# Leaving the last four item groups of a graph-attention edge pass out of gathers, sums, scores and products

## The chip, the cores and the metric

The kernel runs on one core of one Trainium2 chip. The metric is the device time of one execution in microseconds (us): the median of several runs, of the whole program from its first to its last instruction with what the runtime puts around it. Beside the runs stands one execution that the hardware profiler recorded. A measurement of this kernel is repeated and its median compared with that of the kernel before.

## The reference, cut to what matters

A graph-attention layer with a residual, then a layer of experts with a residual. The change touches the attention over the edges only:

```python
def _L0_gnn_ref(x, edge_index, edge_attr, W_l, b_l, W_r, b_r, att, bias):
    N, E, D, H, C = (2500, 40000, 256, 8, 32)
    NEG_SLOPE = 0.2
    n = x.shape[0]
    x_l = (x @ W_l + b_l).reshape(n, H, C)
    x_r = (x @ W_r + b_r).reshape(n, H, C)
    src, dst = (edge_index[0], edge_index[1])
    x_j = x_l[src]
    g = jax.nn.leaky_relu(x_r[dst] + x_j, NEG_SLOPE)
    alpha = jnp.einsum('ehc,hc->eh', g, att)
    alpha = alpha + jnp.log(edge_attr)[:, None]
    amax = jax.ops.segment_max(alpha, dst, num_segments=n)
    ex = jnp.exp(alpha - amax[dst])
    denom = jax.ops.segment_sum(ex, dst, num_segments=n)
    alpha = ex / (denom[dst] + 1e-16)
    out = jax.ops.segment_sum(x_j * alpha[..., None], dst, num_segments=n)
    return out.reshape(n, H * C) + bias
```

The input has 6250 nodes of 256 features and 100,000 edges, sorted by `dst`. So a run of consecutive edges belongs to one node, and a tile of 128 edges touches few tiles of 128 nodes.

## The kernel before, in words

`build` runs one block after another: `prepare` (layer norm, the two projections, the list of items), `edges` (the attention), `route` (second layer norm, gate, slots of tokens), `experts`, `combine`. Between two blocks all engines meet. The change lies in `edges` and in `pipeline`, which lays out its work.

**Items, groups, chunks.** An item is one tile of 128 edges paired with one tile of 128 nodes that it touches. Items come in pairs of edge tiles (`PAIR` = 2). There are `EB` = 391 such pairs and `NODE_TILES` = 49 tiles of nodes; a pair needs one more item pair each time the node tile changes, so at most 2 x (391 + 48) = 878 items can exist. `ITEMS` rounds this up to 896. Four items are a group (`G`), so there are `GROUPS` = 224 groups, and 32 items, or 8 groups (`TURN`), are a chunk: 28 chunks. The last chunk is groups 216 to 223; groups 220 to 223 hold items 880 to 895, which is above 878. Items that do not exist are padding: their weights come out as zero.

**What a group needs.** In the order of the data:

- POOL gathers the left rows of the group's sources, four indirect DMAs (`gather`, L749), 16 groups ahead at most (`RINGS`): it waits on `weighed` of the group 16 back.
- SP loads the right rows of the node tiles (`load_rights`, L764) and the local node numbers (`load_locals`, L771), and for each chunk the marks of runs (`load_chunk`, L781).
- ACT makes the one-hot matrix (`part` L984, `one_hot` L990); PE sums right and left rows (`sum_rows`, L1087 and L1089, in two halves); ACT rectifies (`rectify`, L976).
- DVE multiplies with the attention vector and reduces to scores (`scale` L821, `put_linear` L826, `score` L836).
- When a chunk's eight groups are scored, the running maximum over each run of edges is taken once for the chunk: PE `turn` (L1113), DVE `sweep`, `sweep_back`, `set_ends`, `bind`, `raise_first`, `shift` (L845 to L903), PE `spread_ends` and `turn_back` (L1121, L1130), ACT `exp_weights` (L1039), PE `let_fall` (L1138). The marks reach PE by `spread_mark` (L1102, steps 5, 6 and 7 of a chunk) and are copied by ACT in `keep_mark` (L1003) one step later.
- Then, per group: DVE multiplies left rows by weights (`weigh`, L912), ACT makes the second one-hot matrix (`measure` L1046, four of them, and `mark` L1054, L1057), PE multiplies (`gain`, L1150, two halves), DVE adds each half to the accumulator in SBUF (`add`, L941). At a chunk's first group DVE also rescales the accumulator (L927).

**What sets the order.** Each engine runs a software pipeline: at step c it does each stage of its list for group c + offset. The offsets are written by hand in the calls of `pipeline`: sums at 0, scores at 0, `weigh` at -11, `add` at -13, `gain` at -14. So group g is summed by PE in step g and its products are made in step g + 14; the last step in which PE has both kinds is 223, and steps 224 to 237 have products only. `weigh` may run two groups ahead of `gain` (`W` has two buffers), `gain` one half ahead of `add` (`p_gain` has two).

`pipeline` writes a first stretch of steps straight, then a hardware loop (`Fori`) whose body is 16 steps (`un` = `2 * TURN`), then the rest straight:

```python
    turns = max(first, (steps - max(most, 0)) // un)
    for c in range(-most, first * un):
        at(0, c)
    if turns > first:
        with eng.Fori(first, turns) as i:
            for c in range(un):
                at(i, c)
    for c in range(turns * un, steps - least):
        at(0, c)
```

With offsets above zero (DVE 7, ACT 1, SP 6) the loop ends at step 208 and steps 208 and later are straight. PE and POOL have none, so their loop goes on to step 224 before the change. A step in the straight part has a plain integer as its group number (`g.n`); in the loop it is a register expression.

## Time and profile before

| what | value |
|---|---|
| median of 3 runs | 2026.81 us (2023.36 to 2027.67) |
| the profiled execution: its time | 2019.49 us |
| the profiled execution: span, first to last instruction | 2017.8 us |
| mean granted TensorE clock | 0.941 |
| PE busy | 1780.2 us (88%) |
| DVE busy | 1481.4 us (73%) |
| ACT busy | 1263.4 us (63%) |
| POOL busy | 1202.5 us (60%) |
| `edges`, first gather to last add | 210.8 us to 1416.4 us |

Busy time is time in which an engine worked on an instruction that computes or starts a gather. TensorE has two rows, PE for matmuls and PEld for weight loads, which overlap. A wait is given with the instruction behind it and with what released it ("issue" when nothing that the profile shows did). All times inside the execution are us from the span's start. PEclk is the granted TensorE clock: 1.00 is the upper level (2.4 GHz), 0.50 the lower (1.2 GHz).

### The profile page before, as it was taken

How to read it: one execution, taken by the hardware profiler on the slowest of the kernel's cores; microseconds unless marked ns; L12 is line 12 of the kernel's file. 1: busy time of each engine (PE TensorE's matmuls, PEld its weight loads, DVE VectorE, ACT ScalarE, POOL GpSimd, SP SyncE). 2: the span in 40 equal slices, each digit the busy share in tenths (PEclk: the TensorE clock that was granted, in tenths of full speed). 3: DMA queues.
4: the chain of work that ended last, by engine and by line, in shares of the span. 5: the costliest groups of instructions: out<-in, count | busy, mean ns of one | idle time of the engine just before them, and what ended most of it. 6: DMA issues, size and time to landing. Idle time of an engine off the chain costs nothing. (4 is left out here: it accounts for less than half of the span.)

```text
span 2017.8 us, 41053 instructions
## 1 busy us (share of the span) xinstructions
PE 1780.2 (88%) x9591; PEld 1479.8 (73%) x9592; DVE 1481.4 (73%) x2751; ACT 1263.4 (63%) x3200; POOL 1202.5 (60%) x1314
## 2 busy tenths in 40 slices
PE   5998579999999999999999999997587999999950
PEld 3665467777777877878778787885576999999950
DVE  5554579898998988999889998998876434343325
ACT  1343368898898988989889898997440232323210
POOL 2521677777777777777777777770617555555520
PEclk8899799999999999999999999999558999999985
DMA  5566677787777777778777777770931222222229
GB/s 209 137 205 200 200 235 239 230 238 227 228 241 227 239 224 239 234 222 242 227 232 237 226 239 228 244 233 17 311 112 45 71 70 70 70 70 70 71 78 334
DMA packets 219886, 377.11 MB, mean 187 GB/s; under 512 B 45465, under 2 KB 103813, under 8 KB 219541
## 3 DMA queue, kind: packets, MB, share of 16 engines
q1 hardware_dynamic: 158673, 217.06, 32.7%
q0 software_dynamic: 53760, 150.08, 26.4%
q10 hardware_dynamic: 7284, 8.39, 1.2%
q14 instruction: 147, 1.20, 0.2%
q8 instruction: 22, 0.36, 0.1%
HBM read 321.30 MB, written 55.32 MB: 187 GB/s over the span
## 5 line engine op out<-in xcount | busy, mean ns | idle before, releaser
L749 POOL DMA_INDIRECT rows<-left_rows,idx x896 | 852.8, 952 | 306.7 <-issue 294.1
L1087 PE MATMUL p_row<-rights,hotT 128*128 128x256 f32 x1792 | 516.1, 369 | 45.0 <-DMA rows<-left_rows,idx 23.3
L1089 PE MATMUL p_row<-rows,ident 128*128 128x256 f32 x1792 | 538.5, 382 | 0.0
L1150 PE MATMUL p_gain<-W,hots 128*128 128x264 f32 x1792 | 485.0, 394 | 37.4 <-ACT W L1057 24.5
L1150 PEld LDWEIGHTS p_gain<-W,hots 128*128 128x128 f32 x1792 | 324.8, 189 | 129.5 <-issue 71.3
L1087 PEld LDWEIGHTS p_row<-rights,hotT 128*128 128x128 f32 x1792 | 329.7, 192 | 110.3 <-issue 33.3
L976 ACT ACTIVATE L<-p_row 128x512 f32<-128x512 f32 x448 | 263.4, 588 | 109.8 <-PE p_row L1089 109.1
L912 DVE TENSOR_TENSOR W<-rows,p_weights 128x1024 f32<-128x1024 f32 x224 | 271.8, 1213 | 46.9 <-PE p_gain L1150 46.7
L1046 ACT ACTIVATE far<-iota_row,dl 128x128 f32<-128x128 f32 x896 | 304.9, 391 | 0.0
L821 DVE TENSOR_TENSOR L<-L,p_weights 128x1024 f32<-128x1024 f32 x224 | 270.8, 1209 | 41.6 <-ACT L L976 23.0
L1576 ACT ACTIVATE e_hT<-e_ph,b_column 128x128 f32<-128x128 f32 x420 | 119.7, 368 | 267.5 <-PE e_ph L1601 267.4
L836 DVE TENSOR_REDUCE raw<-L 128x32 f32<-128x1056 f32 x224 | 277.7, 1240 | 1.1
L1089 PEld LDWEIGHTS p_row<-rows,ident 128*128 128x128 f32 x1792 | 278.1, 191 | 0.0
L1601 PE MATMUL e_ph<-e_xT,e_w_own 128*128 128x128 f32 x1680 | 206.9, 277 | 1.2 <-DVE e_w_own L1546 1.2
L1560 DVE TENSOR_TENSOR e_y<-e_py,e_b 128x256 f32<-128x256 f32 x105 | 44.6, 424 | 213.9 <-PE e_py L1612 213.9
L941 DVE TENSOR_TENSOR acc<-acc,p_gain 128x264 f32 x448 | 187.9, 419 | 17.1 <-PE p_gain L1150 9.0
L1601 PEld LDWEIGHTS e_ph<-e_xT,e_w_own 128*128 128x128 f32 x1680 | 198.0, 194 | 1.6 <-DVE e_xT L1553 1.5
L1612 PE MATMUL e_py<-w,e_hT 128*128 x840 | 198.6, 380 | 0.2 <-ACT e_hT L1576 0.2
L1524 POOL DMA_INDIRECT results<-e_y,goes_to x105 | 103.6, 987 | 154.1 <-DVE e_y L1560 154.1
L1054 ACT ACTIVATE hots<-far,unit 128x512 f32<-128x512 f32 x224 | 161.9, 723 | 25.5 <-PE p_gain L1150 6.1
L1612 PEld LDWEIGHTS e_py<-w,e_hT 128*128 128x128 f32 x840 | 151.7, 191 | 16.6 <-issue 0.4
L984 ACT ACTIVATE apart<-locals,iota_column 128x512 f32<-128x512 bf16 x224 | 158.7, 708 | 6.1 <-DMA locals<-item_locals 6.0
(248 smaller groups left out, 1967.3 us busy)
## 6 DMA issues: line engine op xcount, KB each, us to landing
rights<-right_rows SPq DMA_DIRECT2D x448, 256.0 KB
locals<-item_locals SPq DMA_DIRECT2D x112, 256.0 KB, 3.7
rows<-left_rows,idx POOLq DMA_INDIRECT x896
right_rows<-p_parts SPq DMA_DIRECT2D x49, 256.0 KB, 2.2
c_rows<-results SPq DMA_DIRECT2D x12, 1024.0 KB, 13.5
w<-in_L_ffn_W SPq DMA_DIRECT2D x16, 512.0 KB, 6.1
left_rows<-p_y SPq DMA_DIRECT2D x49, 132.0 KB, 2.1
kept_rows<-X SPq DMA_DIRECT2D x7, 896.0 KB, 4.4
```

Of the source, the lines that this page charges most:

```text
L749: nc.gpsimd.indirect_dma_start(out=rows[:, g.slot(RINGS), n, :], out_offset=None, in_=d["left"][:, :], in_offset=bass.IndirectOffsetOnAxis ...
L821: nc.vector.tensor_tensor(own, own, p_weights[:, clear_of, SPAN:SPAN + D].rearrange("p (h c) -> p h c", c=C).unsqueeze(1) .to_broadcast([P ...
L836: nc.vector.tensor_reduce(raw[:, parity(g), :, at:at + 2 * H].rearrange("p u (b h) -> p b u h", h=H), L[:, g.slot(APART), :, :, :].rearran ...
L912: nc.vector.tensor_tensor(W[:, g.slot(2), :, :, 0:C], rows[:, g.slot(RINGS), :, 0:D].rearrange("p n (h c) -> p n h c", c=C), p_weights[:, ...
L941: nc.vector.tensor_tensor(to, to, p_gain[:, n, 0:D + H], ALU.add).then_inc(added, 1)
L976: nc.scalar.activation(L[:, g.slot(APART), PAIR * n:PAIR * (n + 1), :, 0:C].rearrange("p n h c -> p (n h) c"), p_row[:, n, :].rearrange("p ...
L1046: nc.scalar.activation(far[:, n, :], s["iota"][:, :], ACT.Abs, bias=s["dl"][:, bass.ds(g.n * G + n, 1)], scale=-1.0).then_inc(distance, 1)
L1087: nc.tensor.matmul(to, hotT[:, g.slot(2), i, :], rights[:, g.slot(2), n, part * D:(part + 1) * D], start=(part == 0), stop=False)
L1089: last = nc.tensor.matmul(to, s["ident"][:, :], rows[:, g.slot(RINGS), i, 0:D], start=False, stop=True)
L1150: last = nc.tensor.matmul(p_gain[:, n, 0:D + H], hots[:, g.slot(2), i, :], W[:, g.slot(2), i, :, :].rearrange("p h c -> p (h c)"), start=( ...
L1601: last = nc.tensor.matmul(ph[:, g.slot(2), m * P:(m + 1) * P], w1_own[:, g.slot(2), k, m * P:(m + 1) * P], xT[:, g.slot(2), k * P:(k + 1) ...
L1612: last = nc.tensor.matmul(py[:, g.slot(2), 0:D], hT[:, g.slot(2), m * P:(m + 1) * P], w2[:, bass.ds(e, 1), m, :].rearrange("p a f -> p (a ...
```

## The change

`LIVE` is the number of groups that can hold an item: 880 items rounded up from 878, or 220. Two helpers, `idle` and `live`, leave a stage out for a group whose number is an integer of 220 or more. `live` is put around the stages of gathers, loads of rights and locals, one-hot matrices, sums, rectifying, scores, weighing, products and adds. Stages that work once for a chunk (marks, sweeps, exp, rescale) stay for the last chunk too. PE's `turn` of the last chunk waits for the score of group 219 in place of that of group 223. Since only integers can be compared, the last half chunk has to be in the straight part: `pipeline` gets a parameter `unrolled`, and with `TURN` given there the loops of PE and POOL end at step 208, as those of the other engines do.

```diff
@@ -40,6 +40,7 @@
 G = 4
 RING = 4
 GROUPS = ITEMS // G
+LIVE = -(-PAIR * (EB + NODE_TILES - 1) // G)
@@ -105,7 +106,7 @@
-def pipeline(eng, steps, stages, un=UN):
+def pipeline(eng, steps, stages, un=UN, unrolled=0):
...
-    turns = max(first, (steps - max(most, 0)) // un)
+    turns = max(first, (steps - max(most, unrolled)) // un)
...
+        def idle(g):
+
+            return isinstance(g.n, int) and g.n >= LIVE
+
+        def live(stage):
+
+            return lambda g: None if idle(g) else stage(g)
...
-                pipeline(pool, GROUPS, [(0, gather)], 2 * TURN)
+                pipeline(pool, GROUPS, [(0, live(gather))], 2 * TURN, TURN)
...
-                pipeline(sp, GROUPS, [(1, load_rights), (4, load_locals), (6, load_chunk)], 2 * TURN)
+                pipeline(sp, GROUPS, [(1, live(load_rights)), (4, live(load_locals)), (6, load_chunk)], 2 * TURN, TURN)
...
-                pipeline(v, GROUPS, [(0, scale), (0, put_linear), (0, set_open), (1 - SUM, add(0)), (-1, sweep), (0, score),
+                pipeline(v, GROUPS, [(0, live(scale)), (0, live(put_linear)), (0, set_open), (1 - SUM, live(add(0))), (-1, sweep), (0, live(score)),
                                      (-2, bind), (-1, sweep_back), (-2, carry_over), (TURN - 1, list_ahead), (0, empty),
-                                     (-2, raise_first), (-2, raise_last), (-2, shift), (-1, set_ends), (-WEIGH, weigh),
-                                     (1 - SUM, add(1))], 2 * TURN)
+                                     (-2, raise_first), (-2, raise_last), (-2, shift), (-1, set_ends), (-WEIGH, live(weigh)),
+                                     (1 - SUM, live(add(1)))], 2 * TURN)
...
-                pipeline(act, GROUPS, [(-1, keep_mark(0)), (-1, keep_mark(1)), (-1, keep_mark(2)), (1, part), (0, rectify(0)),
-                                       (1, one_hot), (late, measure(0)), (late, measure(1)), (-4, exp_drop), (-3, mark_first),
-                                       (0, rectify(1)), (-4, exp_weights), (late, measure(2)), (late, measure(3)), (-4, lower),
-                                       (late, mark)], 2 * TURN)
+                pipeline(act, GROUPS, [(-1, keep_mark(0)), (-1, keep_mark(1)), (-1, keep_mark(2)), (1, live(part)), (0, live(rectify(0))),
+                                       (1, live(one_hot)), (late, live(measure(0))), (late, live(measure(1))), (-4, exp_drop), (-3, mark_first),
+                                       (0, live(rectify(1))), (-4, exp_weights), (late, live(measure(2))), (late, live(measure(3))), (-4, lower),
+                                       (late, live(mark))], 2 * TURN)
...
-                        wait(pe, scored, g.n + 1)
+                        wait(pe, scored, LIVE if idle(g) else g.n + 1)
...
-                pipeline(pe, GROUPS, [(0, sum_rows(0)), (-2, turn), (-5, let_fall), (-SUM, gain(0)),
-                                      (-3, spread_ends), (-4, turn_back), (0, sum_rows(1)), (-SUM, gain(1)),
-                                      (0, spread_mark(0)), (0, spread_mark(1)), (0, spread_mark(2))], 2 * TURN)
+                pipeline(pe, GROUPS, [(0, live(sum_rows(0))), (-2, turn), (-5, let_fall), (-SUM, live(gain(0))),
+                                      (-3, spread_ends), (-4, turn_back), (0, live(sum_rows(1))), (-SUM, live(gain(1))),
+                                      (0, spread_mark(0)), (0, spread_mark(1)), (0, spread_mark(2))], 2 * TURN, TURN)
```

Nine lines are added above the edge pass, so a line of `edges` after the change stands 9 further down (L912 becomes L921), and one of the blocks before it 1 further down.

How the instructions stand on PE at steps 222 and 223 of the edge pass (sums of groups 222 and 223, products of groups 208 and 209). Before the change the second half of step 223 is the end of the loop body:

```order
L1087 MATMUL p_row<-rights,hotT 128x256 [waits g_rectified]
L1087 MATMUL p_row<-rights,hotT 128x256
L1089 MATMUL p_row<-rows,ident 128x256
L1087 MATMUL p_row<-rights,hotT 128x256 x2
L1089 MATMUL p_row<-rows,ident 128x256
L1150 MATMUL p_gain<-W,hots 128x264 [waits g_added]
L1150 MATMUL p_gain<-W,hots 128x264
L105 REGISTER_ALU
L1102 MATMUL p_back<-marks_by_block,to_blocks 128x256 [waits g_marks_kept]
L123 REGISTER_ALU
L123 COMPARE_AND_BRANCH
```

and with the change, from the product of group 208 on, with no branch behind them:

```order
L1159 MATMUL p_gain<-W,hots 128x264 [waits g_marked,g_added,g_weights_put,g_weighed]
L1159 MATMUL p_gain<-W,hots 128x264
L1159 MATMUL p_gain<-W,hots 128x264 [waits g_added]
L1159 MATMUL p_gain<-W,hots 128x264
L1111 MATMUL p_back<-marks_by_block,to_blocks 128x256 [waits g_marks_kept]
L1159 MATMUL p_gain<-W,hots 128x264 [waits g_marked,g_added,g_weights_put,g_weighed]
L1159 MATMUL p_gain<-W,hots 128x264
L1159 MATMUL p_gain<-W,hots 128x264 [waits g_added]
L1159 MATMUL p_gain<-W,hots 128x264
L1111 MATMUL p_back<-marks_by_block,to_blocks 128x256 [waits g_marks_kept]
```

In steps 220 to 223 PE has the products and the marks only; the rows of sums, six to a half group, are gone.

On DVE, step 220 (scores of group 220, `weigh` of group 209, adds of group 207), before:

```order
L821 TENSOR_TENSOR L<-L,p_weights 128x32x32
L826 TENSOR_TENSOR L<-rows,logw 128x32
L941 ISA
L941 TENSOR_TENSOR acc<-acc,p_gain 128x264
L836 TENSOR_REDUCE raw<-L 128x2x2x8
L912 TENSOR_TENSOR W<-rows,p_weights 128x32x32
L941 ISA
L941 TENSOR_TENSOR acc<-acc,p_gain 128x264
```

and with the change:

```order
L950 ISA
L950 TENSOR_TENSOR acc<-acc,p_gain 128x264
L921 TENSOR_TENSOR W<-rows,p_weights 128x32x32
L950 ISA
L950 TENSOR_TENSOR acc<-acc,p_gain 128x264
```

The two multiplications and the reduction that make a score are gone; the order of what stays is the same.

## Rows read from the trace of the kernel before

**Rows 1.** The page, part 2, its 40 slices: busy tenths, granted clock.

```profile
PE   5998579999999999999999999997587999999950
...
DVE  5554579898998988999889998998876434343325
...
POOL 2521677777777777777777777770617555555520
PEclk8899799999999999999999999999558999999985
```

**Rows 2.** Busy time by stretch; columns: length, busy (instructions) of each engine, clock, DMA.

```profile
1285.00:1300.00 15.00, 15.00 (x81) 12.54 (x80) 13.84 (x23) 14.22 (x35) 11.33 (x12) 1.00 0.81 248
...
1302.00:1342.00 40.00, 39.59 (x209) 32.91 (x208) 38.25 (x62) 36.68 (x90) 30.25 (x33) 1.00 0.78 240
...
1353.00:1373.00 20.00, 19.89 (x103) 16.07 (x102) 18.82 (x28) 17.37 (x44) 7.16 (x8) 1.00 0.51 140
...
1396.00:1416.00 20.00, 14.68 (x58) 9.98 (x56) 13.15 (x22) 11.04 (x32) 0.00 (x0) 1.00 0.00 0
```

**Rows 3.** Timeline of POOL: last gathers, first work of the next block.

```profile
1360.10 0.95 POOL L749 DMA_INDIRECT rows<-left_rows,idx  x1 [0.31 <-issue]
1361.35 0.94 POOL L749 DMA_INDIRECT rows<-left_rows,idx  x1 [0.30 <-issue]
1417.53 9.16 POOL L1236 TENSOR_TENSOR acc<-acc,r_inv 128x256 f32<-128x256 f32 x14 [55.23 <-DVE r_inv L1292]
```

**Rows 4.** Timeline of DVE, from the second add of step 219 on.

```profile
1359.50 0.42 DVE L941 TENSOR_TENSOR acc<-acc,p_gain 128x264 f32 x1
...
1378.34 0.42 DVE L941 TENSOR_TENSOR acc<-acc,p_gain 128x264 f32 x1
...
1415.94 0.43 DVE L941 TENSOR_TENSOR acc<-acc,p_gain 128x264 f32 x1 [0.41 <-PE p_gain L1150]
```

**Rows 5.** The same timeline: one step of the drain, and where it rescales.

```profile
1394.73 0.42 DVE L941 TENSOR_TENSOR acc<-acc,p_gain 128x264 f32 x1
...
1397.97 0.42 DVE L941 TENSOR_TENSOR acc<-acc,p_gain 128x264 f32 x1
...
1400.86 0.42 DVE L941 TENSOR_TENSOR acc<-acc,p_gain 128x264 f32 x1
1401.52 0.43 DVE L941 TENSOR_TENSOR acc<-acc,p_gain 128x264 f32 x1 [0.24 <-DVE acc L941]
1402.60 1.22 DVE L912 TENSOR_TENSOR W<-rows,p_weights 128x1024 f32<-128x1024 f32 x1 [0.65 <-PE p_gain L1150]
1403.73 0.42 DVE L941 TENSOR_TENSOR acc<-acc,p_gain 128x264 f32 x1
```

**Rows 6.** Timeline of ACT in the drain: one step, and a copy of marks.

```profile
1373.87 0.36 ACT L1003 ACTIVATE M<-p_back 128x256 f32<-128x256 f32 x1
...
1403.34 1.28 ACT L1046 ACTIVATE far<-iota_row,dl 128x128 f32<-128x128 f32 x4
1405.47 0.72 ACT L1054 ACTIVATE hots<-far,unit 128x512 f32<-128x512 f32 x1 [0.85 <-PE p_gain L1150]
1406.10 0.24 ACT L1057 ACTIVATE W<-weights 128x32 f32<-128x32 f32 x1
```

**Rows 7.** Timeline at a loop boundary, step 112: ACT, then PE behind it.

```profile
799.85 0.38 ACT L1003 ACTIVATE M<-p_back 128x256 f32<-128x256 f32 x1 [2.86 <-issue]
...
802.07 0.49 PE L1087 MATMUL p_row<-rights,hotT 128*128 128x256 f32 x2 [1.45 <-ACT hotT L990]
```

**Rows 8.** Busy time by stretch, the block behind the edge pass (columns as above).

```profile
1440.00:1480.00 40.00, 40.00 (x207) 40.00 (x206) 34.10 (x130) 30.13 (x75) 16.96 (x31) 0.50 0.89 299
...
1512.00:1543.00 31.00, 28.70 (x176) 22.41 (x175) 30.72 (x132) 0.00 (x0) 27.99 (x41) 1.00 0.00 1
```

**Rows 9.** Weight loads of PE: those of the products in the drain at clock 1.00, those of the gate at 0.50.

```profile
L1150 PEld LDWEIGHTS p_gain<-W,hots 128*128 128x128 f32 x51 | 9.1, 189 | 9.2 <-DVE acc L941 7.5 <-issue 0.5
...
L1446 PEld LDWEIGHTS r_pg<-r_wg,r_xT 128*128 128x128 f32 x153 | 37.2, 334 | 0.0
```

## The prediction

> **What bounds the kernel now.** I read the page's slices first [rows 1]. PE stands at 9 from the seventh slice to the twenty-seventh, 21 slices of 50 us, with the clock at 9: this is the edge pass. DVE stands at 8 or 9 there and POOL at 7. The busy time by stretch [rows 2] tells more: in 40 us of full steps PE is busy 39.59, DVE 38.25 and ACT 36.68. PE sets the pace and DVE is 1.3 us behind it, so taking work from one engine alone would move the time little. The four full steps that the change thins out, 1353 to 1373, look the same (19.89 and 18.82 of 20).
>
> POOL's gathers follow each other every 1.25 us, 5.0 us a group, which is as fast as PE. But the last one starts at 1361.35, and POOL then waits 55.23 us for the next block [rows 3]. So its end is not what ends the pass. The pass ends with the last add of DVE at 1415.94 [rows 4].
>
> From step 224 on nothing is summed, and the products of fourteen groups drain. Here PE is busy 14.68 of 20 us, DVE 13.15, ACT 11.04 [rows 2]: no engine is full, a ring of waits sets the step. DVE's timeline shows it [rows 5]: second add at 1400.86, first add of the next group 0.66 later, `weigh` at 1402.60 after 0.65 of waiting for the product, next second add at 1403.73. A plain drain step lasts 2.87 us; the one with the rescale lasts 3.24 (1394.73 to 1397.97).
>
> **The change, part by part.** I count on DVE, which ends the pass, from its second add of step 219 at 1359.50.
>
> *Steps 220 to 223.* Before, the second add of step 223 starts at 1378.34 [rows 4]: four full steps take 18.84 us. With the change these steps have no score on DVE, no sums on PE and no one-hot matrix for sums on ACT. What stays is what a drain step has: one `weigh`, two adds, two half products, four `measure` and one `mark`. So they run as drain steps: 4 x 2.87 = 11.5 us. Step 221 also rescales, for chunk 26: 3.24 - 2.87 = 0.37.
>
> *The end.* Before, thirteen more second adds follow, for groups 211 to 223: 1415.94 - 1378.34 = 37.60 us. With the change groups 220 to 223 are gone, so nine follow. The four that go are taken at the plain step: 37.60 - 11.5 = 26.1 us. The drain's last two steps, which have no `weigh` any more, stay last ones and are as short as before. The maximum of the last chunk stays in steps 224 to 228 in both kernels, beside the products of the same groups, so its cost is in the 26.1 already.
>
> *Together:* 18.84 + 37.60 = 56.4 us before, 11.5 + 0.4 + 26.1 = 38.0 after: **18.4 us less**. In other words, four full steps go and nothing else; the number of drain steps is the same.
>
> *Marks in thin steps.* PE still spreads three sets of marks, one each in steps 221 to 223, and ACT copies each at the head of its next step, before `measure` and `mark`. ACT then needs 0.36 + 1.28 + 0.72 + 0.24 = 2.60 us from the mark to the end of the step [rows 6], plus the spreading itself and two semaphores; PE wants that `mark` some 2.9 us after the product that stands before the spreading. That is about even. Before, full steps covered it. Bounds: nothing, if PE and ACT just meet, and 3 x 0.36 = 1.1 us if each copy shows whole. I take 0.4, since the margin is near zero and not far below.
>
> *Gathers, loads of rights and locals.* 16 gathers, 8 loads of rights and 2 of locals go. They lie beside PE and end 54 us before the pass ends [rows 3]: 0. The cover is the drain itself, which is still 38 us long. A lighter DMA load speeds nothing in the drain, in which no transfer is awaited.
>
> *The wait of `turn`.* It now asks for the score of group 219, ready some 15 us sooner. Only PE can gain by it, and DVE, on which I count, is busy 18.82 of 20 us just before [rows 2], so it gives nothing: 0. Behind `turn` on PE stand the products of group 211, which wait for `weighed` in any case.
>
> *Loops of PE and POOL end at 208.* Twelve full steps of PE and twelve of POOL are now straight code with waits on constants. Two numbers bound it. On the side of a gain: a loop's return can cost a stall. ACT's does, 2.86 us without any visible reason, and PE stands 1.45 us behind it [rows 7]. PE's own return at step 208 lies between 1285 and 1300, where PE is busy 15.00 of 15.00 us [rows 2], so this return costs nothing and its removal gives nothing. The other bound is a cost of leaving the loop. DVE and ACT leave theirs at 208 too and are busy 13.84 and 14.22 of those 15 us, with no stall of such a size. I take 0 and keep 2.9 us to either side.
>
> The Trainium skill, "Runtime: NRT & Kernel Launch", section "Instruction fetch mechanics", says that a taken branch breaks the sequential prefetch of instructions and can stall the engine until its target is fetched. By that rule PE saves one stall and the sum is 21 us in place of 18. ACT's row agrees with it, PE's does not.
>
> *Everything behind the edge pass* starts earlier and is unchanged, since all engines meet between blocks.
>
> **The sum.** 18.4 - 0.4 = 18.0 us. Against the profiled execution that is 2019.49 - 18.0 = 2001.5, a span of some 1999.8 with the last add at 1398. That execution is 7.3 us faster than the median of the three runs, outside their band, so the saving is carried over to the median: 2026.81 - 18.0 = **2008.8 us**. The part of the execution that is touched is 56 us long, and a spread between executions lies mostly elsewhere, so I see no reason to scale it.
>
> **The rivals.**
>
> *A. Half clock moves in (less gained).* The granted clock is 1.00 through the drain and 0.50 in the block behind it, where PE is busy 40.00 of 40 us [rows 2, 8]; it is back at 1.00 from 1512. If the fall comes early and takes the drain, a weight load takes 334 ns in place of 189 [rows 9], and the four of one half product lie in the ring: 4 x 0.145 x 13 steps = 7.5 us. If instead its rise stays where it was while the work comes 18 us sooner, up to 18 us more of that work run at half: 9 us. Either leaves about 10 us gained: 2017. Against it: the drain is as long and as loose as before, and there the clock held for 43 us.
>
> *B. A loop's return is given back (more gained).* PE's return costs what ACT's does, hidden at step 208 in a way that the rows do not show: 2.9 us more, 2005.9. It is the skill's rule above. Against it stands the full 15.00.
>
> *C. Straight code is supplied too slowly (slower).* PE has no slack in full steps (0.41 of 40 us), so every stall of its instruction supply in steps 208 to 219 is on the path. Price of one: 2.86 us, ACT's. The point from which it decides is 18.0 / 2.86, more than six stalls in twelve steps. With one a step, 12 x 2.86 = 34 us, the time is 2043. Against it: DVE and ACT run their straight steps after 208 with no such gap, and PE was straight from step 224 on already.
>
> *D. The drain steps do not reach 2.87 us at its head (less gained).* ACT and the marks bind, and each of steps 220 to 223 takes 3.9 us, for instance: 4 us given back, 2012.8. ACT at 2.60 of 2.87 us is what speaks for it.
>
> That the change does something else than it says I leave out: the order on PE and DVE shows the removed rows and no others.
>
> **How the numbers follow.** The sum within its bounds (-1.5 to +1 us for marks and pattern) has 0.72; A 0.08; B 0.07; C 0.02; D 0.08; 0.03 is for what I have not seen. The band of the runs shown is 4.3 us wide, so a median can move by 2 us by itself. The range has to reach from B (2005.9, less 2) to D (2012.8, plus 2): 2004 to 2015. A and C are left out with what I have not seen, 0.13 in all. A measurement of this kernel can tell some 0.2%, 4 us, from no change. Faster by more than that: the sum, A, B, D and most of the rest, 0.95. Within it: 0.03. Slower: C, 0.02.
>
> **What would show it.** In the changed profile: 880 gathers, 1760 rows each of L1096, L1098 and L1159 in place of 1792, 220 of each score instruction; the last gather near 1341; DVE's second add of step 219 still near 1359.5; from there plain steps of 2.87 us; the last add near 1398; POOL's wait before the next block about 57 us, 2 us more than before. PE's share in the stretch before 1353 stays at 98% or more. Wrong would be: gaps on PE before L1096 or L1159 "issue" in steps 208 to 219 (C), a clock of 0.50 before the last add (A), DVE steps of 3.5 us or more at 1360 to 1372 with ACT's L1012 copies awaited (D), a last add of step 219 several us sooner (B).

## The result, and the profile after

| | before | after |
|---|---|---|
| median of 4 runs each | 2025.09 us (2021.70 to 2027.67) | 2006.48 us (2003.98 to 2008.39) |
| the profiled execution: time, span | 2019.49, 2017.8 us | 2004.81, 2003.1 us |
| first gather | 210.82 | 212.76 |
| DVE's second add of step 219 | 1359.50 | 1362.74 |
| DVE's second add of step 223 | 1378.34 | 1374.25 |
| last add | 1415.94 | 1399.96 |
| from there to the end of the span | 601.8 us | 603.0 us |

The ratio is 0.9908, 95% interval [0.9887, 0.9930]: 18.6 us less by the medians. Forecast were 18.0 us less and 2008.8 us. In some executions a kernel is slower at a lower granted clock: of the changed kernel's on the third chip of the experiments two took 2028.37 (the profiled one) and 2952.90 us against 1997.72 to 2005.76, and totals are compared without such executions.

The page of the changed kernel, its counts and its slices; the groups are the costliest, with busy us and mean ns of one behind the bar:

```profile
PE 1765.4 (88%) x9495; PEld 1465.1 (73%) x9496; DVE 1464.2 (73%) x2727; ACT 1247.4 (62%) x3160; POOL 1187.3 (59%) x1298
...
PE   5999579999999999999999999997687999999950
...
DVE  5554579998988989889898898997876333334315
...
POOL 2532577776777777777777777760626555555520
PEclk8989689999999999999999999999558999999985
...
L758 POOL DMA_INDIRECT rows<-left_rows,idx x880 | 837.4, 952 | 303.3 <-issue 291.3
L1096 PE MATMUL p_row<-rights,hotT 128*128 128x256 f32 x1760 | 507.0, 370 | 44.7 <-DMA rows<-left_rows,idx 20.3
L1098 PE MATMUL p_row<-rows,ident 128*128 128x256 f32 x1760 | 529.8, 383 | 0.0
L1159 PE MATMUL p_gain<-W,hots 128*128 128x264 f32 x1760 | 478.8, 396 | 34.1 <-ACT W L1066 23.2
```

880 gathers and 1760 of each matmul: the change does what its diff says. The slices look as before [rows 1]. What moved, 19 us in all, is shorter than a slice of 50 us, so the timeline has to show it.

Busy time by stretch of the changed kernel (length, then busy us and instructions of PE, its weight loads, DVE, ACT, POOL; granted clock; share and GB/s of DMA): the first two answer to the first two of [rows 2], the third is steps 220 to 223, the fourth the drain up to the last add, the fifth the half clock of the next block [rows 8].

```profile
1290.00:1305.00 15.00, 15.00 (x82) 12.67 (x81) 13.91 (x22) 14.23 (x35) 11.35 (x13) 1.00 0.84 248
1305.00:1345.00 40.00, 39.49 (x208) 32.45 (x207) 38.04 (x61) 36.70 (x90) 30.24 (x33) 1.00 0.78 237
...
1362.74:1374.25 11.51, 9.63 (x37) 5.95 (x37) 8.51 (x16) 8.65 (x26) 0.00 (x0) 1.00 0.00 1
1374.25:1399.96 25.71, 19.10 (x76) 13.02 (x76) 19.16 (x36) 16.51 (x50) 0.00 (x0) 1.00 0.00 1
1402.60:1498.20 95.60, 68.22 (x336) 66.91 (x337) 76.39 (x279) 43.26 (x105) 40.98 (x67) 0.50 0.66 223
```

DVE's timeline, the thin steps 220 to 223 from the second add of step 219 on (start, length; in brackets the idle time before it and what ended it):

```profile
1362.74 0.41 DVE L950 TENSOR_TENSOR acc<-acc,p_gain 128x264 f32 x1
1363.75 0.43 DVE L950 TENSOR_TENSOR acc<-acc,p_gain 128x264 f32 x1 [0.60 <-DVE acc L950]
1364.47 1.22 DVE L921 TENSOR_TENSOR W<-rows,p_weights 128x1024 f32<-128x1024 f32 x1 [0.29 <-PE p_gain L1159]
1365.61 0.42 DVE L950 TENSOR_TENSOR acc<-acc,p_gain 128x264 f32 x1
1366.29 0.43 DVE L936 SCALAR_TENSOR_TENSOR acc<-p_turn,acc 128x264 f32 x1 [0.26 <-DVE acc L950]
1366.75 0.43 DVE L950 TENSOR_TENSOR acc<-acc,p_gain 128x264 f32 x1
1367.35 1.22 DVE L921 TENSOR_TENSOR W<-rows,p_weights 128x1024 f32<-128x1024 f32 x1 [0.17 <-PE p_gain L1159]
1368.49 0.42 DVE L950 TENSOR_TENSOR acc<-acc,p_gain 128x264 f32 x1
...
1371.37 0.42 DVE L950 TENSOR_TENSOR acc<-acc,p_gain 128x264 f32 x1
...
1374.25 0.42 DVE L950 TENSOR_TENSOR acc<-acc,p_gain 128x264 f32 x1
```

The second adds start at 1362.74, 1365.61, 1368.49, 1371.37 and 1374.25: four steps of 2.87 or 2.88 us, drain steps from the first one on. The step at 1365.61 has the rescale (L936) in it and is not longer: its 0.46 us stand where a plain step waits 0.65 us for PE's product; the wait in front of `weigh` has shrunk to 0.17.

The rescale of the drain, and the last add, in the same timeline:

```profile
1390.64 0.42 DVE L950 TENSOR_TENSOR acc<-acc,p_gain 128x264 f32 x1
1391.31 0.43 DVE L936 SCALAR_TENSOR_TENSOR acc<-p_turn,acc 128x264 f32 x1 [0.25 <-DVE acc L950]
1391.78 0.43 DVE L950 TENSOR_TENSOR acc<-acc,p_gain 128x264 f32 x1
1392.38 1.22 DVE L921 TENSOR_TENSOR W<-rows,p_weights 128x1024 f32<-128x1024 f32 x1 [0.17 <-PE p_gain L1159]
1393.52 0.42 DVE L950 TENSOR_TENSOR acc<-acc,p_gain 128x264 f32 x1
...
1399.96 0.43 DVE L950 TENSOR_TENSOR acc<-acc,p_gain 128x264 f32 x1 [0.41 <-PE p_gain L1159]
```

1390.64 to 1393.52 is 2.88 us, where the same step took 3.24 before [rows 5]. From the second add of step 219 to the last add it is 37.22 us, before 56.44: **19.22 us less**. The other 4.5 us by which the two profiled executions differ less lie elsewhere: the first gather starts 1.94 us later, the stretch from there to step 219 is 1.30 us longer (1149.98 against 1148.68) and the part behind 1.28 us longer. So 14.7 us remain between those two.

POOL's last gather, and its wait before the next block [rows 3]:

```profile
1344.47 0.95 POOL L758 DMA_INDIRECT rows<-left_rows,idx  x1 [0.30 <-issue]
1401.55 2.91 POOL L1245 TENSOR_TENSOR acc<-acc,r_inv 128x256 f32<-128x256 f32 x5 [56.13 <-DVE r_inv L1301]
```

### The profile page after: what moved, and what is told of

It is laid out like the page before. It is cut to its first block and busy times, and to the rows that moved or that the text cites. A ratio compares the mean times of both kernels' runs of the same rounds, so it can differ in the third digit from the quotient of the medians.

```text
span 2003.1 us, 40603 instructions
## 1 busy us (share of the span) xinstructions
PE 1765.4 (88%) x9495; PEld 1465.1 (73%) x9496; DVE 1464.2 (73%) x2727; ACT 1247.4 (62%) x3160; POOL 1187.3 (59%) x1298
## 5 line engine op out<-in xcount | busy, mean ns | idle before, releaser
L758 POOL DMA_INDIRECT rows<-left_rows,idx x880 | 837.4, 952 | 303.3 <-issue 291.3
L1096 PE MATMUL p_row<-rights,hotT 128*128 128x256 f32 x1760 | 507.0, 370 | 44.7 <-DMA rows<-left_rows,idx 20.3
L1098 PE MATMUL p_row<-rows,ident 128*128 128x256 f32 x1760 | 529.8, 383 | 0.0
L1159 PE MATMUL p_gain<-W,hots 128*128 128x264 f32 x1760 | 478.8, 396 | 34.1 <-ACT W L1066 23.2
L1159 PEld LDWEIGHTS p_gain<-W,hots 128*128 128x128 f32 x1760 | 319.0, 190 | 125.7 <-issue 68.1
L1096 PEld LDWEIGHTS p_row<-rights,hotT 128*128 128x128 f32 x1760 | 324.1, 192 | 110.2 <-issue 31.5
L1055 ACT ACTIVATE far<-iota_row,dl 128x128 f32<-128x128 f32 x880 | 299.5, 392 | 0.0
L921 DVE TENSOR_TENSOR W<-rows,p_weights 128x1024 f32<-128x1024 f32 x220 | 266.9, 1213 | 44.4 <-PE p_gain L1159 44.2
L845 DVE TENSOR_REDUCE raw<-L 128x32 f32<-128x1056 f32 x220 | 272.9, 1241 | 1.1
L1098 PEld LDWEIGHTS p_row<-rows,ident 128*128 128x128 f32 x1760 | 273.2, 191 | 0.0
L950 DVE TENSOR_TENSOR acc<-acc,p_gain 128x264 f32 x440 | 184.7, 420 | 18.2 <-PE p_gain L1159 9.3
## 6 DMA issues: line engine op xcount, KB each, us to landing
c_rows<-results SPq DMA_DIRECT2D x12, 1024.0 KB, 13.4
```

The source lines that it names most:

```text
L758: nc.gpsimd.indirect_dma_start(out=rows[:, g.slot(RINGS), n, :], out_offset=None, in_=d["left"][:, :], in_offset=bass.IndirectOffsetOnAxis ...
L845: nc.vector.tensor_reduce(raw[:, parity(g), :, at:at + 2 * H].rearrange("p u (b h) -> p b u h", h=H), L[:, g.slot(APART), :, :, :].rearran ...
L921: nc.vector.tensor_tensor(W[:, g.slot(2), :, :, 0:C], rows[:, g.slot(RINGS), :, 0:D].rearrange("p n (h c) -> p n h c", c=C), p_weights[:, ...
L950: nc.vector.tensor_tensor(to, to, p_gain[:, n, 0:D + H], ALU.add).then_inc(added, 1)
L1055: nc.scalar.activation(far[:, n, :], s["iota"][:, :], ACT.Abs, bias=s["dl"][:, bass.ds(g.n * G + n, 1)], scale=-1.0).then_inc(distance, 1)
L1096: nc.tensor.matmul(to, hotT[:, g.slot(2), i, :], rights[:, g.slot(2), n, part * D:(part + 1) * D], start=(part == 0), stop=False)
```

## The experiments

Twelve runs, on three chips; e5 and e10 are the changed kernel again, e9 is e6 again. Each is compared with the kernel before on the same chip. On the chips of the first and the second four, the kernel before takes 2520 and 2500 us. The longer time lies in the full steps: from the first gather to step 219, e1 takes 1640.2 us, 7.5 a group, where the kernel before took 1148.7 on the first chip, 5.2 a group, and its last steps vary from 4.2 to 11.7 us. The drain and the part behind it take what they took. So the first eight are read by their stretches on DVE, and by totals only where the intervals allow it. On the third chip the kernel before takes 2020.8 us.

The stretches, all between starts of DVE's second adds (rounded one by one, so that a difference of printed starts can be 0.01 off); one profiled execution each:

| kernel | 219 to 223 | 223 to last add | together |
|---|---|---|---|
| before | 18.84 | 37.60 | 56.44 |
| the changed kernel | 11.51 | 25.72 | 37.22 |
| e1, loops unrolled only | 21.25 | 37.62 | 58.87 |
| e2, no sums and scores | 11.50 | 38.32 | 49.82 |
| e3, no products | 18.12 | 26.13 | 44.25 |
| e4, weigh last | 9.08 | 23.40 | 32.48 |
| e5, changed again | 11.52 | 25.72 | 37.23 |
| e6, weigh last in the tail | 8.90 | 23.43 | 32.32 |
| e7, no sums on PE | 17.39 | 38.62 | 56.00 |
| e8, no scores on DVE | 20.56 | 37.23 | 57.80 |
| e9, e6 again | 8.90 | 23.37 | 32.27 |
| e10, changed again | 11.63 | 25.97 | 37.59 |
| e11, no gathers | 18.41 | 38.92 | 57.33 |
| e12, LIVE = 216 | 11.52 | 14.20 | 25.72 |

**e1: only the loops are changed.** All 224 groups keep all their stages; only `unrolled` stays, so that PE and POOL leave their loops at 208, as SP did already.

```diff
-                pipeline(pool, GROUPS, [(0, live(gather))], 2 * TURN, TURN)
+                pipeline(pool, GROUPS, [(0, gather)], 2 * TURN, TURN)
...
-                        wait(pe, scored, LIVE if idle(g) else g.n + 1)
+                        wait(pe, scored, g.n + 1)
```

(`live` goes in the same way around every other stage.)

> All 224 groups are worked as before; only the loops of PE and POOL end at step 208. My theory: no change against the kernel before, within 1.5 us, and DVE needs 57.4 us from the score of group 208 to the second add of step 219, as before. Rival B (a loop's return is given back): 2.9 us less, with PE ahead of that by as much. Rival C (straight code is supplied too slowly): more time, 2.9 us for each stall, with gaps on PE in steps 208 to 219.

2520.27 us against 2520.22, ratio 0.9994 [0.9968, 1.0019]. The steps 221 to 223 take 14.04 us and the drain 37.62, as before (14.04 and 37.60). Step 220 took 7.21 us where 4.80 stood before. Such steps come all over the full steps on this chip, straight or in the loop, and none in the drain; for the same reason the 57.4 us expected up to step 219 can't be read here. The interval reaches from 8 us less to 5 us more, so a cost of leaving the loops of 34 us is excluded by it, a stall of 2.9 us is not; for that size the changed kernel's own stretches speak, below.

**e2: sums and scores go, products stay.** Groups 220 to 223 have no gather, load, sum or score, but are weighed, multiplied and added, with stale rows.

```diff
-                                     (-2, raise_first), (-2, raise_last), (-2, shift), (-1, set_ends), (-WEIGH, live(weigh)),
-                                     (1 - SUM, live(add(1)))], 2 * TURN)
+                                     (-2, raise_first), (-2, raise_last), (-2, shift), (-1, set_ends), (-WEIGH, weigh),
+                                     (1 - SUM, add(1))], 2 * TURN)
```

(and so for `add(0)`, for `measure` and `mark` on ACT, and for `gain` on PE)

> Groups 220 to 223 have no gathers, loads, sums and scores, but keep their weighing, products and adds, so their weights come from scores of an older chunk. My theory (the saving is four full steps turned into drain steps, then four drain steps fewer): only the first half is gained, 18.8 - 11.5 = 7.3 us less than before, and from the second add of step 223 to the last add 37 us remain. Rival (each piece is worth the busy time that it takes from PE): the sums are 16 of the 24 matmuls of a group, two thirds of 18.5, so 12.3 us less.

2496.38 us, ratio 0.9898 [0.9861, 0.9934]. Steps 220 to 223 take 11.50 us, the drain 38.32. The first half of the gain, 7.3 us, comes from the sums and scores alone. The whole is 24 us less (17 to 35 by the interval), where 7 were expected: on this chip a full step is longer (e1 takes 21.25 us for four, and 7.5 a group over the whole pass), so turning four of them into 2.88 us is worth more, by an amount that no run here measures by itself. The drain is 0.7 us longer than before: step 227 took 3.96 in place of 2.88, the rescale step 2.88 in place of 3.24. Step 227 is explained under e11.

**e3: products go, sums and scores stay.** The reverse: groups 220 to 223 are gathered, summed and scored, but neither weighed nor multiplied nor added.

```diff
-                pipeline(v, GROUPS, [(0, live(scale)), (0, live(put_linear)), (0, set_open), (1 - SUM, live(add(0))), (-1, sweep), (0, live(score)),
+                pipeline(v, GROUPS, [(0, scale), (0, put_linear), (0, set_open), (1 - SUM, live(add(0))), (-1, sweep), (0, score),
```

(and so for `gather`, the loads, `part`, `one_hot`, `rectify` and `sum_rows`)

> The other half: groups 220 to 223 are gathered, summed and scored as before, but not weighed, multiplied and added. My theory: steps 220 to 223 stay full (18.8 us between the second adds of steps 219 and 223), and the drain has nine second adds behind them in place of thirteen: 11.2 to 11.9 us less than before. Rival (PE's busy time): one third, 6.2 us less.

2506.79 us, ratio 0.9939 [0.9913, 0.9966]. Steps 220 to 223 take 18.12 us, the drain 26.13: 11.5 less than before. The two halves of the gain add up: 7.34 (e2) and 11.47 (e3) are 18.8 of the 19.2. The total, 13.4 us less, agrees.

**e7 and e8: one engine's share alone.** e7 leaves out only PE's sums of the last four groups; ACT and DVE rectify and score what is in the buffers. e8 leaves out only DVE's scores.

```diff
-                                       (0, live(rectify(1))), (-4, exp_weights), (late, live(measure(2))), (late, live(measure(3))), (-4, lower),
+                                       (0, rectify(1)), (-4, exp_weights), (late, measure(2)), (late, measure(3)), (-4, lower),
...
-                        wait(act, summed, 2 * g.n + n + 1)
+                        wait(act, summed, capped(2 * g.n + n + 1, 2 * LIVE))
```

(e7: every `live` goes but those of PE's sums, the gathers and the loads; `capped` holds a wait's number at what the last real group reaches. e8: every `live` goes but those of `scale`, `put_linear` and `score`.)

> Groups 220 to 223 keep all the work of DVE and ACT, scores and products included, but PE does not sum them and nothing is gathered or loaded for them, so their scores come from an older row. My theory (PE sets the pace, DVE is close behind): between the second adds of steps 219 and 223 DVE is then the bound, 17.5 to 18.3 us in place of 18.8, and the drain stays at 37.6. Rival (PE alone makes a step full): 11.5 to 13 us in place of 18.8.

> Groups 220 to 223 are gathered, summed and rectified, and their products are made, but DVE makes no scores for them (two multiplications and the reduction are left out, their weights come from older scores). My theory: PE stays the bound of steps 220 to 223, 20.2 us on PE, and DVE only loses its lag behind PE at the end, up to 2.3 us of PE's waits there: 56.4 us from the second add of step 219 to the last add become 54 to 56. Rival (DVE's scores are what makes the step long): 7 us less, 49 to 50.

One run each, 2498.19 and 2510.14 us, so only the stretches are read. In e7 steps 220 to 223 take 17.39 us, 1.45 less than before. Busy time in them, the granted clock behind the five engines:

```profile
1836.57:1853.95 17.38, 13.25 (x38) 7.96 (x37) 17.35 (x27) 16.56 (x46) 0.00 (x0) 0.70 0.00 0
```

DVE is busy 17.35 of 17.38 us, PE 13.25: DVE alone holds the steps. The drain is 38.62 where 37.6 was expected. The step behind the four takes 4.68 in place of 3.69, and TensorE's clock stands at 0.50 in it until 1857.3, so this 1.0 us is laid to the clock, without a run that shows it by itself; 0.44 us is left of the gain.

In e8 the first of the four took 7.49, in which PE waits 4.7 us for ACT's part of a product, a long step of this chip as in e1. By it the 57.80 us together lie outside the 54 to 56 expected. The other three take 13.07 against 14.04 before: 0.97 less, at clock 1.00. In them DVE is busy 6.53 us and waits 6.3 for PE's products: here PE holds the steps. Only with both engines thinned (e2) does a step fall to 2.88.

**e11: no gathers and loads.** All else stays for groups 220 to 223, on what lies in the buffers.

```diff
-                            wait(pe, gathered[r], (g.turn(RING) + 1) * (16 * G))
+                            wait(pe, gathered[r], capped((g.turn(RING) + 1) * (16 * G), LIVE // RING * (16 * G)))
```

(and so for the waits on rights and locals; every `live` goes but those of `gather`, `load_rights` and `load_locals`)

> Only the 16 gathers, 8 loads of rights and 2 of locals of groups 220 to 223 are left out; all sums, scores, weighing, products and adds of these groups are kept and work on what is in the buffers. Theory (transfers are hidden in the last steps): second add of step 219 to 223 18 to 21 us, from there to the last add 37 to 38.5 us, 55.5 to 59 together as in the kernel before; the last gather comes some 20 us sooner (5 us a group) or 28 us sooner (7 us a group). Rival (a lighter load of transfers is where part of the gain comes from): second add of step 219 to 223 below 16 us.

On the third chip: 2022.34 us, ratio 0.9997 [0.9980, 1.0014]. Transfers are worth nothing there that is seen: steps 220 to 223 are 0.4 us shorter, all of it in step 220 (4.37 against 4.80), whose length varies by as much elsewhere (4.20 in e3, with its gathers). Its drain, from its timeline of DVE, has one step that before has not:

```profile
1392.19 0.42 DVE L954 TENSOR_TENSOR acc<-acc,p_gain 128x264 f32 x1
1393.64 0.43 DVE L954 TENSOR_TENSOR acc<-acc,p_gain 128x264 f32 x1 [1.02 <-PE p_gain L1163]
1395.26 1.22 DVE L925 TENSOR_TENSOR W<-rows,p_weights 128x1024 f32<-128x1024 f32 x1 [1.19 <-PE p_gain L1163]
1396.40 0.42 DVE L954 TENSOR_TENSOR acc<-acc,p_gain 128x264 f32 x1
```

Step 227, 4.21 us, where DVE waits 1.02 and 1.19 us for PE. It is all of the 1.3 us by which this drain is longer, and it is the step that took 3.96 in e2. The granted clock is at its lower level there. Busy time of PE, its weight loads, DVE, ACT and POOL, then the clock, in the 2.9 us ahead, in the 3.4 us of the low clock and in the step 227 of the kernel before:

```profile
1388.40:1391.30 2.90, 1.76 (x10) 1.11 (x9) 2.01 (x4) 2.71 (x10) 0.00 (x0) 1.00 0.00 0
1391.60:1395.00 3.40, 3.40 (x9) 2.59 (x10) 1.45 (x3) 2.50 (x8) 0.00 (x0) 0.50 0.00 0
...
1386.10:1388.97 2.87, 2.40 (x12) 1.87 (x12) 1.98 (x4) 2.84 (x11) 0.00 (x0) 1.00 0.02 6
```

A matmul of the products takes 561 ns on average in this step and 412 in the step of the kernel before. In e2 the clock falls in the same step, from 1870.7 to 1874.1. So the lower level can take a step of the drain, and costs 1.1 to 1.3 us when it does. It took none in the kernel before and in the changed kernel; nothing here says what decides it.

**e4, e6 and e9: `weigh` behind the second add.** A drain step has slack on every engine, and the row [rows 5] shows `weigh` between two adds. These kernels are the changed one with `weigh` behind the second add: e4 in every step, e6 and e9 only for groups from 209 on, that is from step 220. The whole computation is kept.

```diff
+        def late(g):
+
+            return isinstance(g.n, int) and g.n >= LIVE - WEIGH
+
+        def only(when, stage):
+
+            return lambda g: stage(g) if late(g) == when else None
...
-                                     (-2, raise_first), (-2, raise_last), (-2, shift), (-1, set_ends), (-WEIGH, live(weigh)),
-                                     (1 - SUM, live(add(1)))], 2 * TURN)
+                                     (-2, raise_first), (-2, raise_last), (-2, shift), (-1, set_ends), (-WEIGH, live(only(False, weigh))),
+                                     (1 - SUM, live(add(1))), (-WEIGH, live(only(True, weigh)))], 2 * TURN)
```

> The changed kernel with one stage moved: in DVE's step, weigh stands behind the second add, not ahead of it. The computation is whole. My theory (a ring of waits sets the drain step: second add, product of the next group, weigh waits for it, next second add): the wait of 0.65 us before weigh goes and PE makes both half products beside it; the drain step falls from 2.88 to about 2.2 us, 13 steps, so 5 to 10 us less than the changed kernel, some 24 to 28 less than the one before. Rival (DVE's second add then waits for the product instead, or POOL's gathers, which wait for weigh, come later and slow the full steps): no gain, or up to 5 us more than the changed kernel.

> The changed kernel with weigh moved behind the second add in the thin steps only (groups 209 and later). The computation is whole. My theory: the full steps stay as in the changed kernel, and from the second add of step 219 to the last add it takes 32.5 us in place of 37.2, since each step of the drain loses its wait ahead of weigh: 4 to 5 us less than the changed kernel. Rival (what the moved stage gave in the drain came from PE being late at step 219): no difference to the changed kernel.

> The changed kernel with weigh behind the second add from group 209 on, once more, beside e10. Theory (in the drain the product half waits on the second add, weigh stands between): second add of step 219 to last add 32.3 us, 4.9 us less than e10's 37.2, and nothing elsewhere, so the whole differs from e10 by 5 us or 0.2%. The 10 us between the medians of the first pair would then be half noise. Rival (the tail order helps outside the drain too): 8 to 12 us between the medians again, with a difference in front of step 219.

e4: 2512.51 us, ratio 0.9971 [0.9945, 0.9996], 7 us less than before where 24 to 28 were expected; the end is 4.7 us shorter (32.48 against 37.22), but the full steps are longer: 1660.9 us from the first gather to step 219, where e1, e2 and e3 on the same chip take 1640.2, 1630.1 and 1644.7. One execution each, so the size is uncertain. e6: 2464.38 us, 0.9856 [0.9815, 0.9896]. e9: **1994.58 us** (1994.02 to 1996.85, 4 runs), ratio 0.9860 [0.9835, 0.9884]: less than both kernels take. The medians of e5 and e6 lie 10.1 us apart, those of e10 and e9 6.8; the stretch gives 5 of either, and the rest is taken for scatter. The timeline of DVE in e9's drain, second add to second add:

```profile
1386.23 0.43 DVE L958 TENSOR_TENSOR acc<-acc,p_gain 128x264 f32 x1 [0.21 <-DVE acc L958]
1386.57 1.21 DVE L929 TENSOR_TENSOR W<-rows,p_weights 128x1024 f32<-128x1024 f32 x1
1387.70 0.42 DVE L958 TENSOR_TENSOR acc<-acc,p_gain 128x264 f32 x1
1388.34 0.43 DVE L958 TENSOR_TENSOR acc<-acc,p_gain 128x264 f32 x1 [0.21 <-PE p_gain L1167]
1388.68 1.22 DVE L929 TENSOR_TENSOR W<-rows,p_weights 128x1024 f32<-128x1024 f32 x1
```

Here `weigh` starts 0.34 us after the second add, with no wait for PE in front of it, and the step is 2.11 us. Busy time in this step:

```profile
1386.23:1388.34 2.11, 2.02 (x9) 1.44 (x9) 1.90 (x4) 2.08 (x8) 0.00 (x0) 1.00 0.00 0
```

ACT is busy 2.08 and PE 2.02 of 2.11 us: with the ring shortened, these two are nearly full. Other steps of this drain are longer, 2.58 and 2.88 us. In the other order `weigh` stood for 0.65 us waiting for the product, and the second add, whose release PE's next half wants, stood behind `weigh`.

**e5 and e10: the changed kernel again.**

> The changed kernel once more, as the base for the other runs beside it on one chip. My theory: between the second adds of DVE's steps 219 and 223 11.5 us, from there to the last add 25.7 us, whatever the chip does in the full steps ahead of that, and at least 18 us less than the kernel before. Rival (the saving depends on how fast the gathers run): those two stretches come out longer where the full steps are slower.

> The changed kernel as it is. Theory: second add of step 219 to 223 11.5 us, from there to the last add 25.7 us, 37.2 together, on whatever chip; the whole at 0.988 to 0.993 of the kernel before. If the chip runs the full steps in 5.0 us, the whole is 18 to 20 us less than before; if in 7 us, 18 to 26 us less, since a full step is worth more there.

e5: 2474.51 us, 0.9897 [0.9854, 0.9940]. e10: ratio 0.9898 [0.9878, 0.9918], which is 20.6 us of 2020.8; its times from 1997.72 to 2005.76 us all lie above e9's. In its profile the upper level of TensorE's clock is granted at 0.95 in place of 1.00, and the stretches at the end are 0.4 us longer.

**e12: LIVE = 216.** Groups 216 to 219, which hold items, are left out too.

```diff
-LIVE = -(-PAIR * (EB + NODE_TILES - 1) // G)
+LIVE = 216
```

> LIVE is 216 in place of 220: groups 216 to 219, which do hold items, are left out too. Theory (each group left out is worth its full step, the number of drain steps stays): the stretch from the second add of step 215 to the last add is 37.2 to 38 us (eight thin steps of 2.87, then five drain adds of 14.2), against 58.2 of e5 and 57.4 of the changed kernel's first profile: 20 us less. The gain is then linear in the groups left out, 4.7 to 5.1 us each. Rival (the first thin steps lean on work that the full steps ahead had done, so a longer thin stretch is worth less, as when the chunk's weights at steps 216 to 221 come too late): above 42 us.

1981.95 us, ratio 0.9804 [0.9778, 0.9829]: 19.0 us below e10 by the ratios. From the second add of step 215 to the last add it takes 39.22 us (57.37 in the changed kernel), 1.2 above what was expected. Steps 216 and 217 take 3.68 and 4.08 us: the sweeps of the chunk before fall there, as they do at 224 and 225 in all kernels, and I had priced them as plain ones. The rival's 42 us are not reached. So four more groups are worth 18.2 us on DVE, after 19.2 for the first four: 4.5 us each, where 4.7 to 5.1 were expected.

## Why the prediction was right

The two large terms came as forecast and for the reason given; the small ones for marks and rescale did not come. Point by point, on DVE's second adds:

- **Steps 220 to 223.** 11.5 us forecast, 11.51 measured, and e2 gives the same 11.50 with these stages alone. That PE and DVE bound these steps together, which [rows 2] had said by 39.59 and 38.25 of 40 us, is shown by e7 and e8: thinned alone, PE's side gives 1.45 us (0.4 with the clock's fall behind it) and DVE's about 1, both give 7.3. The stretch that the prediction read for these steps, 1353 to 1373, fits PE's; between DVE's own adds, 1359.50 to 1378.34, PE was busy 16.40 and DVE 17.66 of 18.84 us, so DVE is the fuller one there, as e7 says.
- **The rescale of step 221.** 0.37 us forecast, 0 measured. The step that failed is "3.24 - 2.87 = 0.37": it was taken from the only rescale step of the old drain. In the changed kernel neither rescale costs anything, the second one (in the 26.1) included. The rescale step of the drain is 3.24 us in the kernel before, e1, e3, e7 and e11, 2.88 in the changed kernel, e2 and e8. The first kind still scores groups 220 to 223 on DVE, the second kind doesn't. In the kernel before, the 0.36 us stand in front of `weigh`: ACT's `mark`, which waits for the same product, starts at 1396.46, `weigh` only at 1396.84, where in the changed kernel both start together (1392.37 and 1392.38). The five kernels with the longer step have the same instructions on DVE up to there, while their work on PE, POOL and ACT differs. So it goes with what DVE's program holds ahead of this step and not with the rescale itself. What in it costs the time is open.
- **The end.** 26.1 us forecast, 25.72 measured, and e3 has 26.13, with the rescale step at 3.24. That the four plain steps go and nothing else is shown; the 0.4 is the rescale again.
- **Marks.** 0.4 us forecast, 0 measured: the thin steps have no excess. ACT's copies are there and start early enough. Its timeline from the first copy to the second:

```profile
1364.61 0.38 ACT L1012 ACTIVATE R<-p_back 128x256 f32<-128x256 f32 x1 [2.34 <-PE p_back L1111]
1364.89 1.26 ACT L1055 ACTIVATE far<-iota_row,dl 128x128 f32<-128x128 f32 x4
1366.19 0.72 ACT L1063 ACTIVATE hots<-far,unit 128x512 f32<-128x512 f32 x1
1366.81 0.25 ACT L1066 ACTIVATE W<-weights 128x32 f32<-128x32 f32 x1
1367.49 0.39 ACT L1012 ACTIVATE M<-p_back 128x256 f32<-128x256 f32 x1 [0.43 <-PE p_back L1111]
```

  From copy to copy it is 2.88 us, and ACT still waits 0.43 of it. The price of 2.60 us for its work was right; that the margin was "near zero" was not.
- **Gathers and loads.** 0 forecast; e11 has a ratio of 0.9997 and 18.41 us for steps 220 to 223. The last gather came at 1344.47, forecast 1341.
- **The wait of `turn`.** 0 forecast. Before, PE waited 1.23 us for the score of group 223 at `turn` (1377.35); now it waits for nothing there (1372.84), and the next step of DVE takes 3.69 us in both. Elsewhere PE, with no sums left to do, has come to wait: 1.05 us for ACT's `low`, at 1357.0, before the second add of step 219. It is covered: the stretch from the score of step 208 to that add takes 57.52 us, before 57.38.
- **The loops.** 0 forecast. The same stretch holds all twelve new straight steps and the old place of the return, and is 0.14 us longer. e9 and e11 have 56.85 and 56.80 there, so some 0.7 us are the scatter of this stretch, and a stall of 2.9 us is excluded. Rival C (a stall in each step, 34 us) falls by this and by e1. Rival B (2.9 us more gained) isn't seen either: PE is busy 15.00 of 15 us over step 208 with the loop and 15.00 of 15 without. ACT's return costs 2.86 us [rows 7], and it is not the only one. The waits of the kernel before from 300 to 1350 us (us in total, times, longest), of ACT and of PE:

```profile
ACT M L1003 <- issue: 32.3, 11, 3.2
...
PE p_row L1087 <- ACT hotT L990: 16.7, 11, 1.8
PE p_row L1087 <- issue: 1.2, 1, 1.2
```

  ACT's eleven stand 83 us apart, which is 16 steps: one a return. Behind each of them PE waits for the one-hot matrix that ACT makes late, 16.7 us in all, nearly what the whole change gained. DVE has eight such waits, 18.5 us. So the returns that cost are those of ACT and DVE, which the change leaves as they are; no run here takes them out. The Trainium skill, "Runtime: NRT & Kernel Launch", section "Instruction fetch mechanics", says that a taken branch can stall an engine; ACT's rows agree with it, PE's show 1.2 us once.
- **Rival A.** Through the thin steps and the drain of the changed kernel the clock stands at 1.00. In e2 and e11 it falls to 0.50 in step 227, so the rival's mechanism exists, at 1.1 to 1.3 us a fall and not the 7.5 of a whole drain. The half level begins 2.6 us after the last add, before 4.0 us after it, and lasts 95.6 us (1402.6 to 1498.2) where it lasted 92.2 (1419.9 to 1512.1). So it moved with the work. The part behind the edge pass is 1.28 us longer in this profile, and 602.5, 602.9 and 601.8 us long in e9, e11 and e12: no more than its scatter.
- **Rival D.** No thin step is above 2.88 us.

The errors of the sum all point one way: they are costs that did not come, 0.4 for the marks and twice 0.37 for the rescale. Without them the sum is 19.1, and the stretch gave 19.2. The runs gave 18.6 and 20.6, with intervals about 4 us wide to either side, so that 18.6 lies closer to the forecast than the stretch does is chance.

## What to carry to other kernels

Work that is padding costs what its step costs, not what its instructions cost, and a pipelined group costs twice: once where it is a full step, of which the difference to a thin one is saved (7.3 us for four), and once as a step of the drain (11.5 us). Read both from the timeline of the engine that ends last, second add to second add. Where two engines are within 4% of each other, work has to go from both: either one alone gave 1.5 us or less of 7.3. And when a stretch comes out with no engine full, look at what stands in front of the instruction that releases the next engine: moving `weigh` behind the add cut a plain step of the drain from 2.87 to 2.11 us; in the full steps it gained nothing (e4). And look at every engine's loop returns: here they cost ACT 3 us each and PE's own next to nothing.

## What was not expected

**The same kernel took 23% more on other chips**, and 463 of the 467 us between the two profiled executions lie between the first gather and step 219. Busy time by stretch over 400 us of full steps, first the changed kernel in its first profile, then e5's:

```profile
800.00:1200.00 400.00, 380.80 (x1977) 311.79 (x1975) 366.32 (x581) 353.53 (x857) 293.00 (x308) 1.00 0.77 232
```

```profile
1000.00:1400.00 400.00, 314.65 (x1434) 251.07 (x1433) 266.92 (x419) 256.44 (x618) 215.95 (x227) 0.88 0.58 169
```

308 gathers in 400 us against 227, 232 GB/s against 169, no engine full, and a granted clock of 0.88 in place of 1.00. In e5's waits of PE between 1000 and 1200 us the largest are for ACT's and DVE's part of a product (W), up to 6.2 us at a time, where 0.9 us is the largest in the first. The drain, which moves nothing, takes 37.22 and 37.23 us in the two. So the loss comes only where transfers run beside the work. Whether the transfers are slower themselves, whether instructions come later, or what part the lower clock has in it or only follows from the waits, no run here tells.

**A short fall of the clock** stands in the changed kernel at 1358.2 to 1361.6 us, at step 219, before the thin steps; the kernel before has none there. The steps around it took 4.20 us (218 and 219 each; before 4.20 and 4.25), so it cost nothing to be seen: DVE is busy through both of them, and PE, whose sums are done, only 2.94 us of step 218.
